# Windowed attention: weighing in four column strips, scores in two row halves, one projection a step, the maximum subtracted on GpSimd

## The reference

```python
q = (x @ Wq + bq).reshape(B, S, H, hd).transpose(0, 2, 1, 3)      # H = 16, hd = 16
k = (x @ Wk + bk).reshape(B, S, H, hd).transpose(0, 2, 1, 3)
v = (x @ Wv + bv).reshape(B, S, H, hd).transpose(0, 2, 1, 3)
scores = jnp.einsum('bhqd,bhkd->bhqk', q, k) * scale
scores = jnp.where(allowed, scores, NEG_INF)                      # j <= i and i - j < 64
attn = jax.nn.softmax(scores, axis=-1)
out = jnp.einsum('bhqk,bhkd->bhqd', attn, v)
out = out.transpose(0, 2, 1, 3).reshape(B, S, D)
return out @ Wo + bo
```

## Time and profile before

| | |
|---|---|
| time, median of 3 runs | 1192.36 us (1190.61 to 1192.55) |
| the profiled execution | 1186.31 us, its span 1184.5 us |
| mean granted TensorE clock | 0.946 |
| busy share of PE, DVE, ACT, POOL | 88%, 54%, 37%, 48% |
| attention, first to last scores | 57.6 to 279.6 us |
| first matmul after the attention | 294.1 us |

### The profile page before, as it was taken

How to read it: one execution, slowest core, us unless ns; L and a number is a source line. 1 busy time by engine, 2 the same in 40 slices (tenths; PEclk the granted TensorE clock), 3 DMA queues, 4 the chain that set the end, 5 groups by cost and what they waited for, 6 DMA issues and landing times. The chain is left out here.

```text
span 1184.5 us, 24732 instructions
## 1 busy us (share of the span) xinstructions
PE 1042.7 (88%) x7478; PEld 863.1 (73%) x7496; DVE 642.9 (54%) x1548; ACT 438.1 (37%) x1149; POOL 572.3 (48%) x754
## 2 busy tenths in 40 slices
PE   8699999998884699999999998479998957988996
PEld 6467777777673499999999998236555536888995
DVE  2487777775679577644444442677999651110111
ACT  2255555553244344444444441122332223323331
POOL 0183333331050578877777754777776002333332
PEclk9799999997998899999999998788999977999998
DMA  6100000000100576677898862334455012456342
GB/s 229 39 1 1 0 0 0 0 1 1 56 21 1 179 211 209 200 229 232 231 250 255 238 189 88 103 94 111 113 146 213 19 45 54 142 198 208 99 127 72
DMA packets 81174, 136.33 MB, mean 115 GB/s; under 512 B 19372, under 2 KB 58031, under 8 KB 78672
## 3 DMA queue, kind: packets, MB, share of 16 engines
q0 software_dynamic: 19584, 52.60, 17.0%
q1 hardware_dynamic: 32144, 55.90, 14.4%
q10 hardware_dynamic: 29376, 27.01, 6.6%
HBM read 195.35 MB, written 36.05 MB: 195 GB/s over the span
## 5 line engine op out<-in xcount | busy, mean ns | idle before, releaser
L1226 POOL DMA_INDIRECT x_x<-m_x_rows,x_idx x200 | 195.4, 977 | 67.1 <-issue 51.8
L1245 PE MATMUL x_pup<-x_xt,x_w 128*128 128x128 f32 x1600 | 212.6, 276 | 0.2 <-DMA x_w<-in_experts 0.2
L1245 PEld LDWEIGHTS x_pup<-x_xt,x_w 128*128 128x128 f32 x1600 | 195.7, 193 | 0.8 <-DMA x_w<-in_experts 0.6
L1491 POOL DMA_INDIRECT rl_y<-m_y_rows,rl_idx x136 | 135.6, 997 | 44.2 <-issue 36.6
L1309 DVE TENSOR_TENSOR x_hid<-x_gate,x_pup 128x128 f32<-128x128 f32 x200 | 57.7, 288 | 161.7 <-ACT x_gate L1281 158.8
L427 POOL TENSOR_TENSOR wa_kheads<-wa_kT,cst 128x544 f32<-128x544 f32 x64 | 73.0, 1150 | 133.2 <-PE wa_scores L506 87.5
L1254 PE MATMUL x_pdown<-x_w,x_hid 128*128 128x256 f32 x400 | 119.4, 381 | 0.2 <-DVE x_y L1316 0.2
L1277 ACT ACTIVATE x_xt<-x_pturn 128x256 f32<-128x256 f32 x200 | 76.7, 383 | 91.1 <-PE x_pturn L1237 83.3
L2232 DVE TENSOR_TENSOR x_y<-x_pdown,late_b 128x256 f32<-128x256 f32 x24 | 10.2, 425 | 172.7 <-PE x_pdown L2176 172.7
L2164 PE MATMUL x_pup<-x_xt,late_w 128*128 128x128 f32 x768 | 92.3, 280 | 11.7 <-DMA late_b<-in_b 9.3
L2164 PEld LDWEIGHTS x_pup<-x_xt,late_w 128*128 128x128 f32 x768 | 90.6, 195 | 15.9 <-issue 15.2
(11 more groups left out here) (281 smaller groups left out, 1866.9 us busy)
## 6 DMA issues: line engine op xcount, KB each, us to landing
x_w<-in_experts SPq DMA_DIRECT2D x200, 384.0 KB
late_w<-in_w SPq DMA_DIRECT2D x52, 1024.0 KB, 12.1
m_y_rows<-x_y ACTq DMA_DIRECT2D x200, 128.0 KB
m_x_rows<-xn SPq DMA_DIRECT2D x34, 128.0 KB, 1.8
x_x<-m_x_rows,x_idx POOLq DMA_INDIRECT x200
late_b<-in_b SPq DMA_DIRECT2D x24, 128.0 KB
patches<-in_patches SPq DMA_DIRECT2D x3, 864.0 KB, 12.4
rl_y<-m_y_rows,rl_idx POOLq DMA_INDIRECT x136, 2.8
```

Source lines behind the costliest of these rows:

```text
L1226: nc.gpsimd.indirect_dma_start(x[:, s, :], None, x_rows, bass.IndirectOffsetOnAxis(ap=idx[:, s:s + 1], axis=0))\
L1245: mm = nc.tensor.matmul(pup[:, bank, m * P:(m + 1) * P], w[:, s, (m * DC + c) * I0:(m * DC + c + 1) * I0], xt[:, s, c * P:(c + 1) * P], st ...
L1491: nc.gpsimd.indirect_dma_start(y[:, t % YR, kk, :], None, y_rows, bass.IndirectOffsetOnAxis(ap=idx[:, n:n + 1], axis=0))\
```

## The change

Four things change within `window_attention`.

The scores. The keys are spread four heads at a time: `kheads` has only four copies of 68 columns, and the upper 64 rows hold heads 0 to 3, the lower 64 heads 4 to 7. Four matmuls of 136 columns over 64 rows each take the place of two of 272 over 128 rows; they alternate between the lower and the upper half of the rows, and each half writes its own bank.

The weighing. The values, padded with zeros to 32 columns for each head (`vals`, `head_cols`), are now the weights, and the turned probabilities (68 columns) the moving side. Head m writes to 32 rows of `pout` of its own, m modulo 4, so that there are four strips; heads 4 to 7 add to the strips of heads 0 to 3 in the other 16 rows. A second pass with a matrix of ones in place of the values gives the sums, each repeated over the 16 rows of its head. The result stands transposed, as `aT` needs it, so `out` and its transpose go; the order of the heads' rows changes, and `Wo` and `bv` are laid out by `head_rows` on the host. VectorE's reciprocal and multiplication are now 128 x 68, and ScalarE places `outs` straight from it (`placed`).

The jobs. `JOBS` gives each step one projection, always between the scores and the turning: k1, q1, the four values, k0, q0 (the last two for the next block).

The engines. GpSimd subtracts the maximum (`shift`), one unit behind the spreading of keys. VectorE adds the output bias, two tiles a step of the first block, and clears `vals` and `ones` at the start of the stage.

The core of the diff:

```diff
+    TILE = 2 * HD
+    BANK = HC // 2 * TILE + HD
...
-        kheads = sb("kheads", [P, 2, HC, S])
-        vals = sb("vals", [S, ABLK, H, VW])
+        kheads = sb("kheads", [P, 2, HC // 2, S])
+        vals = sb("vals", [S, ABLK, 2 * DC * BANK])
+        ones = sb("ones", [S, 3 * HD])
...
+        JOBS = [("k1", 1), ("q1", 1), ("v", 0), ("v", 1), ("v", 2), ("v", 3), ("k0", 0), ("q0", 0)]
...
+                def shift(unit, slot4, slot2):
+                    pool.wait_ge(peaked, unit + 1)
+                    nc.gpsimd.tensor_tensor(probs[:, slot4, :, :], probs[:, slot4, :, :],
+                                            peak[:, slot2, :].unsqueeze(2).broadcast_to([S, HC, S]),
+                                            ALU.subtract).then_inc(shifted, 1)
...
+                        if not (isinstance(blk, int) and blk == 0 and step == 0):
+                            shift(blk * UNITS + step - 1, (step - 1) % 4, (step - 1) % 2)
...
-                    for hd in range(HC):
-                        mm = nc.tensor.matmul(pout[0:S, hd * VW:(hd + 1) * VW], probsT[:, slot2, hd, :],
-                                              vals[:, img, c * HC + hd, :], start=True, stop=True)
+                    for sums in range(2):
+                        for hd in range(HC):
+                            rows = slice(hd % (HC // 2) * TILE, (hd % (HC // 2) + 1) * TILE)
+                            late = hd // (HC // 2)
+                            of = ones[:, late * HD:late * HD + TILE] if sums else vals[:, img, head_cols(c, hd)]
+                            mm = nc.tensor.matmul(pout[rows, sums * S:(sums + 1) * S], of, probsT[:, slot2, hd, :],
+                                                  start=(late == 0), stop=(late == 1))
...
-                        for g in range(2):
-                            bank = pscore[0:S, step % 2, g, 0:4 * S]
-                            mm = nc.tensor.matmul(bank, qT[:, c, b * S:(b + 1) * S],
-                                                  kheads[:, step % 2, 4 * g:4 * g + 4, :].rearrange("p m n -> p (m n)"),
+                        for quarter in range(4):
+                            m, g = quarter // 2 * 2, quarter % 2
+                            half = slice(g * P // 2, (g + 1) * P // 2)
+                            mm = nc.tensor.matmul(pscore[0:S, step % 2, g, m * S:(m + 2) * S], qT[half, c, b * S:(b + 1) * S],
+                                                  kheads[half, step % 2, m:m + 2, :].rearrange("p m n -> p (m n)"),
                                                   start=True, stop=True)
...
-                    nc.vector.reciprocal(invsum[:, slot, :], out3[:, :, HD]).then_inc(inverted, 1)
+                    nc.vector.reciprocal(invsum[:, slot, :], pout[:, S:2 * S]).then_inc(inverted, 1)
                     dve.wait_ge(inverted, unit + 1)
-                    nc.vector.tensor_tensor(outs[:, slot, :].rearrange("q (m v) -> q m v", v=HD), out3[:, :, 0:HD],
-                                            invsum[:, slot, :].unsqueeze(2).broadcast_to([S, HC, HD]),
-                                            ALU.mult).then_inc(normalised, 1)
+                    if not early:
+                        dve.wait_ge(placed, unit - 1)
+                    nc.vector.tensor_tensor(outs[:, slot, :], pout[:, 0:S], invsum[:, slot, :], ALU.mult)\
+                        .then_inc(normalised, 1)
...
-                        dve.wait_ge(peaked, unit + 1)
-                        nc.vector.tensor_tensor(probs[:, step % 4, :, :], probs[:, step % 4, :, :],
-                                                peak[:, step % 2, :].unsqueeze(2).broadcast_to([S, HC, S]),
-                                                ALU.subtract).then_inc(shifted, 1)
```

More of the change, by code:

```diff
@@ L348, in window_attention @@
         pjob = s_attn.enter_context(nc.psum_tensor("wa_job", [P, 512], fp32))
[L349 to L352, removed]
+        (block_copied, keys_spread, vals_set, scored, masked, turned, weighted, jobs_done, jobs_moved, placed,
+         peaked, shifted, exped, turn_moved, inverted, normalised, biased, ones_all) = sems(
+            nc, k, "wa", "block_copied keys_spread vals_set scored masked turned weighted jobs_done "
+            "jobs_moved placed peaked shifted exped turn_moved inverted normalised biased ones_all")
         def four(ap):
             return ap.rearrange("q (g m) n -> q g m n", g=2)
[L359 to L382, removed]
+        JOBS = [("k1", 1), ("q1", 1), ("v", 0), ("v", 1), ("v", 2), ("v", 3), ("k0", 0), ("q0", 0)]
+        first_jobs, mid_jobs = list(enumerate(JOBS)), list(enumerate(JOBS))
+        last_jobs = list(enumerate(JOBS[:-2])) + [None, None]
+        n_first, n_mid = len(JOBS), len(JOBS)
         PRO = 2
@@ L440, in _ @@
                 blocks(pool, body)
+                shift(NBLK * UNITS - 1, 3, 1)
             @block.tensor
@@ L457, in do_job @@
                     pe.wait_ge(jobs_moved, job_count(blk, n))
-                    if kind == "out":
-                        unit = blk * UNITS + which - 4
-                        pe.wait_ge(normalised, unit + 1)
-                        nc.tensor.transpose(pjob[:, 0:S], outs[:, which % 2, :], ident[0:S, 0:S]).then_inc(jobs_done, 1)
-                    elif kind == "v":
+                    if kind == "v":
                         if which == 0:
@@ L495, in body @@
                         c, b = step // ABLK, step % ABLK
-                        before, behind, late = table[step]
-                        if before:
-                            do_job(blk, *before)
+                        if step == 0:
+                            pe.wait_ge(jobs_moved, job_count(blk, 0))
                         pe.wait_ge(keys_spread, blk * UNITS + step + 1)
@@ L552, in body @@
                             dve.wait_ge(turned, unit - 3)
+                        if not (start and step < 2):
+                            dve.wait_ge(shifted, unit - 1)
                         nc.vector.tensor_tensor(four(probs[:, step % 4, :, :]), scores,
```

99 lines of the change are left out of this document (49 added, 50 removed).

## The result

The changed kernel takes 1154.11 us, the median of 5 runs (1144.72 to 1155.44), against 1192.46 for the kernel before in 5 runs of the same session. The ratio is 0.963, with an interval of 0.960 to 0.967: 38 us less, where 11 were forecast. The profiled execution took 1144.72 us with a span of 1142.9; that of before took 1186.31.

The account below looks back on a forecast made before the run. TensorE was taken to bound windowed attention, its step falling from 3.59 to 3.4 us: 9.6 us over 48 middle steps plus 1.5 in the first block, 11 in all, giving 1181 us; range 1147 to 1226.

Parts of the forecast that it names:

- rival A: TensorE's step: array packs better than assumed, 2.75 or 2.94 us a step, 34 to 44 us less, 1148 to 1158; chance 0.17.
- the weighing: TensorE's 32 passes over four strips: partial overlap, 17 pass lengths, 0.97 us; full overlap 0.46, none 1.82 or more.
- the step of 3.37: TensorE's step in windowed attention: 0.57 + 0.92 + 0.48 + 0.97 + 0.43 us, against 3.59 before.
- Scores: Scores in two array halves: partial overlap, five pass lengths instead of eight, 0.57 us against 0.91 before.
- Changes of shape: TensorE between strips, halves and whole array: three changes a step, 0.10 us each plus exposed loads, 0.43 in all.
- Projection and turning: TensorE's step: a projection keeps its 0.92 us and turning the probabilities its 0.48.
- The handovers of 0.26 a step: Waits around the single bank `pjob`: 0.26 us a step, said to go with one projection a step.
- VectorE and GpSimd: Work beside TensorE's step: VectorE 2.3 us (3.2 in the first block), GpSimd 1.7, worst 2.7; all hidden.
- little to spare: GpSimd's key spreading and the path from scores to exp: hidden, but only just if the step fell to 2.8 us.
- First block: First block of windowed attention: earlier first scores and evening help, VectorE's additions may cost something; -1.5 us.
- Last block and tail: End of windowed attention: last block about the same; tail trades four output turns for longer reciprocals, 0.
- Rival D: TensorE's clock: it pauses three times a step, and the clock fell to 0.59 where it waited before; chance 0.05.

Follow-up runs that it names:

- e1: Changed kernel with the weighing's sixteen matmuls ordered one strip after the other: 1193.75 us, ratio 0.997 to the kernel before.
- e5: Changed kernel with the two matmuls of each strip next to each other in the weighing: ratio 0.966 to the kernel before.
- e2: Changed kernel with scores over the whole array again, two matmuls of 272 columns over 128 rows: 1172.74 us, ratio 0.981 to the kernel before.
- e6: Changed kernel with the weighing ahead of the turning, four changes of shape a step instead of three: ratio 0.966 to the kernel before.
- e10: Changed kernel with projections at the old steps (two at steps 0 and 1, one at 2 to 5): ratio 0.979 to the kernel before.
- e4: Kernel before with one projection a step, all behind the scores, turned output kept: 1210.12 us, ratio 1.012 to the kernel before.
- e3: Changed kernel with VectorE subtracting the maximum and GpSimd adding the bias, as before: 1162.85 us, ratio 0.973 to the kernel before.
- e7: Changed kernel in which the spreading of a new block's keys waits for one job less: ratio 0.963 to the kernel before.
- e11: e8 with the copy of the next block's columns moved from GpSimd to VectorE: ratio 0.968 to the kernel before.
- e12: e11 with the scores of two units back to back at every second step: 1297.72 us, ratio 1.016 to the kernel before.
- e8: e7 with VectorE adding the bias one tile a step in the first and last blocks: 1220.57 us, ratio 0.958 to the kernel before.
- e9: Changed kernel run once more with no edit, on another chip: ratio 0.964 to the kernel before.

## Why the prediction was wrong

The direction was right, 1154 lies within the range of 1147 to 1226, and the mechanism is rival A, which I gave 0.17 and 1148 to 1158. The forecast was wrong by its size: 11 us, where 38 were measured.

*The step that failed is the weighing.* I took the passes of one matmul in one strip to hold up everything behind them except the next one's first, 17 lengths or 0.97 us. The 32 passes start within 0.46 us: the first passes of the four strips start within 0.02 us, and each strip's next passes 0.06 to 0.08 later. The strips overlap fully, then. This is 0.51 of the 0.60 us by which the step of 3.37 missed the measured 2.77 (near the mean of 2.71 and 2.81, with one projection of either kind). A bound that I had worked out was the truth, and I chose between the ends by an analogy that no row supported. The order of the program does hold passes back, but only once some three wait in one strip (e1, e5). The written order hops to another strip with every matmul, two passes each, and so never meets that limit. Had I asked how the order visits the strips, rival A would have had the greater chance.

The four strips start 32 passes within 0.46 us. A strip that runs alone starts one each 0.059 us (e1), which is 1.89 one by one, so they are four times as fast in the written order. But e1 has the same sixteen matmuls in 1.24.

*Scores.* The same mistake, at a fifth of its weight. The passes start in pairs, one in each half, and each pair is worth 0.116 us. Four are 0.46, where I had 0.57 for the bare work. With the change of shape it is 0.62 against my 0.67. e2 prices the halves at 0.26 to 0.30 a step.

*Changes of shape.* I had 0.43 for three, from the earlier trace rows. The bare work of the step, 0.46 for scores and weighing each, 0.92 and 0.48, is 2.32, which leaves 0.39 to 0.49. One more change costs 0.12 (e6). This term was right. The loads bear out that the gaps come with the shape, as I read it in the earlier trace rows. In the changed kernel the loads of the weighing, the scores and the projection start together with their matmuls (148.64, 149.25 and 149.87), while that of the turning, which has the projection's shape before it, starts 0.23 us ahead (150.66 for 150.89). In e2, where the scores have the projection's shape, the projection's load too starts 0.23 ahead (148.75 for 148.98). In e6 the loads of all four groups start with their matmuls (148.46, 149.07, 149.66 and 150.28).

*Projection and turning.* They take 0.92 and 0.48 plus the loads that a change exposes, as forecast. The handovers of 0.26 a step around the bank are gone, as forecast too. e10 shows them come back with the old places, and e4 that evening alone gains nothing.

*VectorE and GpSimd.* Reciprocal 0.581 (0.63 forecast), multiply 0.229 (0.25), subtraction 1.11 (1.10), spreading 0.65 (0.6). VectorE's step is 2.25 us of 2.81, and TensorE paces the middle blocks. e3 shows that VectorE has this room only through the move of the subtraction: without it VectorE would set 2.92. So the move, which I put at nothing, is worth some 11 us in the middle blocks at the true pace; with the bias, which went to VectorE in return, the stage gains 8.

*What the text said would be tight.* At a step of 2.8 the keys of a new block were to have "little to spare". They come late in each block, and the step is 0.46 us longer for it. One half of this is a wait on one job more than the spreading needs (e7). The other stays without the keys being late, where the loop goes round (e11); its cause is not shown.

*First block.* I gave it -1.5 us, and it gave -0.9. I gave VectorE 3.2 us a step there by additions of 0.42. Eight of the sixteen there had to wait for GpSimd's instructions, two together took up to 2.14 us instead of 0.84, and TensorE waits 1.0 and 1.6 us for keys. The sum had the two engines run side by side, though the 0.85 of the earlier trace rows beside the 0.72 of the earlier trace rows showed that they don't always.

*Last block and tail.* I put both at nothing. They gave 4.4 and 4.1 us, a fifth of the stage's gain. The last block is paced by TensorE like the others and gets its shorter steps. In the tail of the kernel before, TensorE waited for VectorE before each of the four turned outputs (1.32 us and three times 0.71):

```profile
282.93 0.35 PE L527 MATMUL wa_job<-cst,wa_outs 68*128 68x68 f32 x1 [1.32 <-DVE wa_outs L541]
```

These are gone, and the granted clock is 0.50 for 6 us of the tail instead of 11. No run takes the two apart. e1, whose strips overlap little, still has a tail of 12.3 us instead of 15.2, so most of this part isn't due to the strips. Where the prediction read nine tenths for TensorE up to the tenth slice, the row has eight in the tenth; that slice holds the tail.

*Luck.* That 1154 also lies in A's own band is in part chance. A counted 52 steps and no tail; the last block and the tail gave more than it allowed, while the keys' waits, the 6.8 us at half clock and 3 us more behind the stage took some back.

*Rival D.* It came small and once: 6.8 us at a granted clock of 0.50 behind the longest waits, in one of three profiles with these waits. e12, with a mean of 0.80 over its stage, shows that it was no idle rival.

*Open.* The timed runs of the change lie between 1144.72 and 1155.44, with a median 9 us above the profiled one; the traces don't tell why. The stage is 43 us shorter, the medians differ by 38. Why the stages behind attention took some 80 us longer on the other two chips is open too. And the gain of e8 over the change is read from the stage alone.

## What to carry to other kernels

When small matmuls are put side by side in strips of the array, write the order so that neighbours in the program go to different strips: the same matmuls took 0.46 us in one order and 1.24 in the other. Where a range has both ends worked out and no row of the trace between them, give the chance to both ends rather than the middle, and look at the order of issue before weighing them. When the pacing engine gets faster, redo the sum of every other engine at the new pace, and look at each wait on a count for one job too many. Where the mean of an instruction lies above its median, look at what the other engines do during the long ones before moving work between engines.

## What the runs showed of the hardware

- The starts of passes in column strips of 32 fit passes that are handed out in program order, with about three waiting in a strip behind the running one: with eight in a row for each strip, the next strip's first starts beside the fifth (e1, 150.57 and 150.56), and four in a row cost 0.04 us a step (e5). One strip took a 68-column f32 pass each 0.059 us, two strips together one each 0.03, and four strips 32 passes in 0.46 (the changed kernel).
- One more change between strips, halves and the whole array in a step cost 0.12 us, with the load that it exposes (e6).
- A tensor_tensor of VectorE with both operands in SBUF and a tensor_tensor or copy of GpSimd held each other up. An addition of 256 columns took 0.41 us where GpSimd stood idle. In 9 of 17 (the changed kernel and e9), 10 (e7) and 13 (e8) it started during one of GpSimd's and took 0.65 to 1.37, until 0.28 us after that one's end, or the end of one right behind it. Elsewhere GpSimd's took longer instead: its subtraction 1.54 instead of 1.09 (the changed kernel), and its spreading of keys 1.63 instead of 0.64 beside two additions of 0.41 that started 0.39 and 0.72 us into it (e9). VectorE's subtraction of 544 columns took 0.72 and up to 1.52 (before). An addition of 256 columns with one operand in PSUM took 0.41 to 0.42 (`h` with `m_pup`, GpSimd idle), and reading scores from PSUM for the mask stayed at 0.72 beside GpSimd.
- In e12 TensorE waited 22 times, 34.9 us in all, and the mean granted clock of its stage was 0.80 instead of 0.96: for the same matmuls it was busy 221.1 us instead of 180.3. Behind two waits of 1.0 and 1.6 us the granted clock was 0.50 for 6.8 us in one execution of three (the changed kernel), and stayed at 1.00 in the other two (e9, e5).
